# Rotary embedding in a transformer layer: the sine product and the value copy move from VectorE to GpSimd

## The reference

```
q = q * cos + rotate_half(q) * sin     # rotate_half: pairs (a, b) -> (-b, a)
k = k * cos + rotate_half(k) * sin
scores = q @ k.T / sqrt(8); softmax; @ v; then @ Wo + bo
```

## Time and profile before

| | |
|---|---|
| median of 3 runs | 843.28 us |
| lowest and highest | 841.11 and 844.68 us |
| span of the profiled execution | 841.5 us |
| TensorE busy | 740.7 us (88%) |
| VectorE busy | 460.5 us (55%) |
| ScalarE busy | 373.8 us (44%) |
| GpSimd busy | 188.6 us (22%) |

### The profile page before, as it was taken

How to read it: one execution, slowest core, us unless ns; L and a number is a source line. 1 busy time by engine, 2 the same in 40 slices (tenths; PEclk the granted TensorE clock), 3 DMA queues, 4 the chain that set the end, 5 groups by cost and what they waited for, 6 DMA issues and landing times.

```text
span 841.5 us, 13291 instructions
## 1 busy us (share of the span) xinstructions
PE 740.7 (88%) x4776; PEld 393.5 (47%) x4776; DVE 460.5 (55%) x942; ACT 373.8 (44%) x569; POOL 188.6 (22%) x158
## 2 busy tenths in 40 slices
PE   4547999999998588999999999996645999999998
PEld 2224656566565333333343444543323565665655
DVE  6314554555456987799978887645313333333334
ACT  6213334344343747646666676776202232222322
POOL 1017333433434513000000000001013333333332
PEclk9877999999998679999999999997967999999999
DMA  5794444434430000000000000000694222122122
GB/s 167 40 29 138 137 122 114 123 113 122 120 89 26 1 1 1 1 1 1 1 2 1 1 2 1 1 2 1 19 28 90 69 75 75 50 75 75 55 70 76
DMA packets 16169, 44.37 MB, mean 53 GB/s; under 512 B 2658, under 2 KB 5090, under 8 KB 16132
## 3 DMA queue, kind: packets, MB, share of 16 engines
q1 hardware_dynamic: 12388, 33.65, 21.2%
q10 hardware_dynamic: 3744, 10.23, 4.0%
HBM read 40.58 MB, written 1.19 MB: 50 GB/s over the span
## 4 chain that ended last, share of the span: by engine, by line
PE 78%; DMA 8%; DVE 6%; ACT 4%; SPq 2%; issue 1%; POOL 1%; DVEq 0%; ACTq 0%; POOLq 0%
PE psum L861 49%; PE psum L1025 8%; DMA R<-oT 8%; PE psum L1009 7%; PE psum L998 7%; PE psum L996 2%; SPq L361 2%; PE psum L1012 2%; DVE m_part L811 2%; PE psum L983 1%; ACT kT L567 1%; ACT xT L474 1%; PE psum L1032 1%; DMA x_res<-x_dram 1%; DVE kaug L801 0%
## 5 line engine op out<-in xcount | busy, mean ns | idle before, releaser
L861 PE MATMUL psum<-xT,W_hi 128*128 128x512 f16 x880 | 266.3, 385 | 0.0
L383 POOL TENSOR_TENSOR R<-R 128x512 f32<-128x512 f32 x112 | 151.4, 1354 | 346.2 <-DVE R L722 237.5
L861 PE MATMUL psum<-W_hi,R 128*128 (+1 forms) x896 | 168.9, 278 | 53.9 <-DVE R L722 53.9
L811 DVE TENSOR_REDUCE m_part<-psum 128x1 f32<-128x512 f32 (+3 forms) x384 | 188.2, 551 | 42.3 <-PE psum L998 40.0
L708 DVE SCALAR_TENSOR_TENSOR R<-psum,R 128x512 f32<-128x512 f32 x108 | 74.6, 691 | 209.5 <-ACT R L495 209.5
L495 ACT ACTIVATE R<-psum 128x512 f32<-128x512 f32 x108 | 64.3, 596 | 246.9 <-PE psum L861 246.9
L582 ACT ACTIVATE R<-psum 128x1024 f32<-128x1024 f32 x144 | 141.8, 1024 | 68.1 <-PE psum L1009 45.7
L861 PE MATMUL psum<-xT,W_lo 128*128 128x512 f16 x440 | 168.5, 383 | 0.0
L861 PEld LDWEIGHTS psum<-xT,W_hi 128*128 (+1 forms) x880 | 87.1, 99 | 83.9 <-issue 4.2
L861 PEld LDWEIGHTS psum<-W_hi,R 128*128 128x128 f16 x896 | 89.1, 99 | 78.6 <-issue 37.2
L861 PE MATMUL psum<-W_lo,R 128*128 (+1 forms) x448 | 124.5, 278 | 0.0
(11 more groups left out here) (101 smaller groups left out, 456.4 us busy)
## 6 DMA issues: line engine op xcount, KB each, us to landing
R<-coef_dram SPq DMA_DIRECT2D x60, 256.0 KB, 3.9
w_stage<-w_dram ACTq DMA_DIRECT2D x26, 384.0 KB, 3.0
R<-coef_dram SPq DMA_DIRECT2D x8, 448.0 KB, 3.5
R<-coef_dram SPq DMA_DIRECT2D x8, 384.0 KB, 3.4
R<-coef_dram SPq DMA_DIRECT2D x6, 320.0 KB, 3.5
R<-coef_dram SPq DMA_DIRECT2D x6, 192.0 KB, 3.8
x_res<-x_dram SPq DMA_DIRECT2D x8, 128.0 KB, 2.2
R<-oT SPq DMA_DIRECT2D x4, 256.0 KB, 16.7
```

The costliest lines, as they stand in the source:

```text
L383: nc.gpsimd.tensor_tensor(hc[:, c, :], v[:, j, c, :], C[:, j, c * CH:(c + 1) * CH], ALU.mult).then_inc(s_hc[c], 1)
L811: nc.vector.tensor_reduce(m_part[:, h, kc:kc + 1], ps[:, 0:n], axis=AX.X, op=ALU.max).then_inc(free_of(e), 1)
L861: ins = nc.tensor.matmul(o, stat(a, k), mov(b, k), start=first and n == 0, stop=last and n == 3 * k_parts - 1, **kw)
```

## The change

GpSimd makes the product with the sine (pairs exchanged) itself, in front of the one with the cosine, and copies the values behind its addition. VectorE keeps the eviction with the bias, and its eviction waits for the copy of the values two tiles earlier (`s_vals`), which comes behind the rotation, in place of `s_rot`. GpSimd waits for its own memset of `qaug` (`s_ready` at 2) ahead of the first tile; VectorE's wait for `s_ready` at 1 goes. The planner's costs of `pj` become 0.6 for VectorE and 3.6 for GpSimd, from 1.2 and 1.8. With these figures the planner's list differs in 22 of its 721 places, all between the 37th and the 61st.

```diff
--- before.py
+++ after.py
@@ -110,7 +110,7 @@
         if kind == "va":
             return [(DVE, 3.2)], []
         if kind == "pj":
-            return [(PE, 1.0), (DVE, 1.2), (POOL, 1.8)], [("sp", t - 2)]
+            return [(PE, 1.0), (DVE, 0.6), (POOL, 3.6)], [("sp", t - 2)]
         if kind == "sp":
             return [(ACTE, 0.9), (DVE, 0.7)], [("pj", t)]
         if kind == "kx":
@@ -424,11 +424,17 @@
             for c in range(NC):
                 pool.wait_ge(s_y[c], MT)
             nc.gpsimd.memset(qaug[:, :, :, 24:32], 0.0).then_inc(s_ready, 1)
+            pool.wait_ge(s_ready, 2)
             for t in range(TT):
 
                 taken(pool, ("pj", t))
                 if t >= 2:
                     pool.wait_ge(s_qklo, t - 1)
+                x = qkv[:, t % 2, 0:QW + KW].rearrange("p (h n e) -> p h n e", n=HD // 2, e=2)
+                sin = rope[:, 1, t, :].rearrange("p (n e) -> p n e", e=2).unsqueeze(1)\
+                    .to_broadcast([P, NH + NKV, HD // 2, 2])
+                nc.gpsimd.tensor_tensor(rot_b[:, t % 2].rearrange("p (h n e) -> p h n e", n=HD // 2, e=2),
+                                        x[:, :, :, ::-1], sin, ALU.mult).then_inc(s_swap, 1)
                 cos = rope[:, 0, t, :].unsqueeze(1).to_broadcast([P, NH + NKV, HD])
                 ra = rot_a[:, t % 2, :]
                 nc.gpsimd.tensor_tensor(ra.rearrange("p (h d) -> p h d", d=HD),
@@ -437,6 +443,9 @@
                 pool.wait_ge(s_pool, 2 + t)
                 pool.wait_ge(s_swap, t + 1)
                 nc.gpsimd.tensor_tensor(ra, ra, rot_b[:, t % 2], ALU.add).then_inc(s_rot, 1)
+                nc.gpsimd.tensor_copy(vals[:, t, :, 0:HD],
+                                      qkv[:, t % 2, QW + KW:QKV].rearrange("p (h d) -> p h d", d=HD)
+                                      ).then_inc(s_vals, 1)
 
             pool.wait_ge(s_xn, 2 * TT)
             for t in range(TT):
@@ -777,22 +786,10 @@
                 elif kind == "pj":
                     ps = filled(dve, e)
                     if t >= 2:
-                        dve.wait_ge(s_rot, t - 1)
+                        dve.wait_ge(s_vals, t - 1)
                     nc.vector.scalar_tensor_tensor(out=qkv[:, t % 2, :], in0=ps[:, 0:QKV], scalar=1.0 / WS,
                                                    in1=bias[:, 0:QKV], op0=ALU.mult,
                                                    op1=ALU.add).then_inc(free_of(e), 1)
-                    taken(dve, e)
-                    if t == 0:
-                        dve.wait_ge(s_ready, 1)
-                    nc.vector.tensor_copy(vals[:, t, :, 0:HD],
-                                          qkv[:, t % 2, QW + KW:QKV].rearrange("p (h d) -> p h d", d=HD)
-                                          ).then_inc(s_vals, 1)
-
-                    x = qkv[:, t % 2, 0:QW + KW].rearrange("p (h n e) -> p h n e", n=HD // 2, e=2)
-                    sin = rope[:, 1, t, :].rearrange("p (n e) -> p n e", e=2).unsqueeze(1)\
-                        .to_broadcast([P, NH + NKV, HD // 2, 2])
-                    nc.vector.tensor_tensor(rot_b[:, t % 2].rearrange("p (h n e) -> p h n e", n=HD // 2, e=2),
-                                            x[:, :, :, ::-1], sin, ALU.mult).then_inc(s_swap, 1)
                 elif kind == "sp":
                     dve.wait_ge(s_qkhi, t + 1)
                     q = rot_a[:, t % 2, 0:QW].rearrange("p (h d) -> p h d", d=HD)
```

## The result

The changed kernel takes 846.29 us in the median of 13 runs (845.07 to 848.5), the kernel before 842.69 us in 13 runs beside it. The ratio is **1.0042 (95% interval 1.0032 to 1.0053)**: slower by 3.6 us, where +2.5 was forecast. The profiled execution spans 845.3 us against 841.5. On TensorE L967 and L980 are the transposes of keys and queries, L995 and L1006 the products for the maxima and the scores, L1022 the value product. (An experiment's own kernel can have other numbers for the same lines; the rows name the tiles.)

What follows compares the result with a forecast made beforehand. TensorE carries 78% of the chain of waits, VectorE 6%; the changed stretch is four stages with different limits. Terms 1.4 - 0.3 + 0 + 1.0 + 0.4 = +2.5 us on the median 843.28 gave 845.8 us, range 841.2 to 850.6.

Steps and rivals of the forecast that it cites:

- The opening: First tiles, up to the first row maximum: GpSimd replaces VectorE as the limit, first maximum at 296.5 us, +1.4 us.
- The pitch of 3.0: Opening stage: time per tile becomes 3.0 us against 2.90, set by GpSimd's four instructions in line plus contention.
- contention 0.25: Opening stage: GpSimd loses 0.25 us per tile to VectorE's two subtractions slipping between, bounds 0 to 0.63.
- The two rivals on GpSimd's price: Opening: reversed read dear, 1.74 us, total 850.3, chance 0.15; full exclusion, 0.63 us lost per tile, total 847.4, chance 0.13.
- Tile 6: Around 303 us: VectorE saves some 1.2 us, but ScalarE's line lets only 0.3 through to the query evacuation, -0.3 us.
- Tile 7: Around 317 us: VectorE's saved 1.2 us ends inside ScalarE's unbroken line up to the query evacuation, 0 us.
- The rival that put the time on the other side: Tiles 6 and 7: VectorE's relief sets the time because ScalarE has room, -2.75 us, total 840.5, chance 0.15.
- The order: Planner's places 37 to 61: second value product in front delays kx 4, +1.0 us; ends -0.7 and +1.1.
- The lower clock level: TensorE: lower clock lasting elsewhere than 306 to 310 us would show the prediction wrong; no term given.
- The bias add: Behind tile 7: GpSimd's bias add ends as VectorE's two subtractions come, lengthening them, +0.4 us; 0 to 0.9.
- The sum: Whole kernel: 1.4 - 0.3 + 0 + 1.0 + 0.4 = +2.5 us, giving 845.8 us; chance of this forecast 0.45.
- Everything behind keeps its order and moves along: Rest of the kernel behind the changed stretch: no further cost, so the span of 841.5 becomes 844.0 us.

Runs made afterwards that it cites:

- e1: The changed kernel with the planner's old costs for `pj`, so the old order of events; 1.0014 against the kernel before.
- e3: The changed kernel with GpSimd's sine product made a second time, into an unread buffer, for tiles 0 to 5; 1.0076 against the kernel before.
- e4: The kernel before, old order, with only tiles 6 and 7 rotated and their values copied as in the change; ratio 0.9997.
- e12: The kernel before, old order, with tiles 0 to 5 rotated by VectorE alone and tiles 6 and 7 by GpSimd alone; ratio 0.9974.
- e6: The kernel before, old order, with tiles 0 to 5 rotated by VectorE alone, tiles 6 and 7 shared as before; ratio 0.9987.
- e7: The kernel before with one planner event moved: the second value product ahead of m 31, `pj` 7 and kx 4; ratio 1.0023.
- e2: The kernel before with only the planner's new costs for `pj`, so the new order, rotation and copy still on VectorE; ratio 1.0026.
- e5: The kernel before, old order, with all eight tiles rotated by VectorE alone; ratio 1.0020.
- e8: The kernel before with the planner's new costs, but the second value product put back behind kx 4; ratio 1.0008.

## Why the prediction came out right

- **The opening** was forecast at +1.4 us and is +1.28 (17.91 - 16.63). The pitch of 3.0 was 2.97. Its parts: the sine product 0.82 by the step, 0.82 by the starts (285.31 to 286.13); contention 0.25, measured 1.09 - 0.87 = 0.22, all of it from L797, none in the addition. The two rivals on GpSimd's price fall by the same rows: 0.863 us for the reversed read, and 0.22 instead of 0.63 us lost to the turns. The 0.05 us by which an instruction starts ahead of its predecessor's recorded end was assumed; the eight bias adds quoted for it give 0.02 (5.84 - 5.70 over seven steps), and the rows after give 0.04 (286.17 against 286.13).
- **Tile 6**, -0.3: measured -0.26, in the change, e1, e3, e4 and e12 alike. A part of the relief went before ScalarE could hide it: L821, with 16 elements, took 0.88 us instead of 0.23 beside GpSimd's products. Of the 1.2 us TensorE's transposes got 0.63 (9.57 us behind the first maximum instead of 10.20), and ScalarE's line let 0.26 through.
- **Tile 7**, 0: measured 0.00 (3.98 in both). The rival that put the time on the other side stands on this step and is refuted by e4.
- **The order**, +1.0 with ends at -0.7 and +1.1, was mis-sized. The two profiles show 12.20 - 11.69 = +0.51, but the 11.69 holds 3.4 us of the lower clock. The same old order at the full clock took 10.66 (e6), the new one 12.20 three times over: **+1.5 us at equal clock**. About 1.1 us of that is the value product (1.10 in e7). The rest comes from the early score products, behind which the maxima's products stand, a half that the sum had at nothing. (Alone and at the lower clock the halves add 1.10 and 0.64 us, 0.2 more than both together at the full clock.) The timed runs give the order +2.2 (e2).
- **The lower clock level** was named in the prediction as what could make it wrong, and had no term. In the change it falls in the two stages ahead of m 32: +0.39 and +1.60 us (four score products and a value product alone 1.86 + 1.94 - 1.02 - 1.07 = 1.71). In the kernel before it falls at 337 us, and by 345 us 0.84 us net is paid back: m 32 is 3.88 us later in the trace (328.48 - 324.60), the value product behind that place 3.04 (348.30 - 345.26). The 3.88 and the 3.04 both hold 0.36 us that was there at the first eviction (278.87 - 278.51). With the 1.03 us that the kernel before loses in the kx 4 stage (11.69 - 10.66) the clock's net by 345 us is 0.39 + 1.60 - 0.84 - 1.03 = 0.12 us: in this stretch both profiles have 6.8 us of the lower level, in other places.
- **The bias add**, +0.4: wrong, it is 0. L452 ends at 322.82 + 5.52 = 328.34, and L797 comes at 329.68 with 0.41 us, undisturbed, because the lateness of everything else had grown past the 2.1 us reckoned.
- **The sum.** Up to 345 us the change costs 1.28 - 0.26 + 0 + 0.51 + 0.39 + 1.60 - 0.84 = 2.68 us, where +2.5 was forecast. Split by cause it is opening 1.28, tile 6 -0.26, order 1.54 at equal clock, clock 0.12, bias add 0. So the order was half a microsecond dearer than its term and the bias add 0.4 cheaper, and these two errors cancel by luck; the clock, unpriced, happened to cost nearly nothing up to here. (The 1.54 and the 1.03 rest on e6's one profile at the full clock.) "Everything behind keeps its order and moves along" did not hold to the end: TensorE's products of equal number are 3.04 us apart at 345 us, 3.3 from 400 to 550, 3.5 at 590 and 3.8 at the end, so 0.8 us more comes behind the change's own stretch. e2 shows the same, +1.6 us at 345 and +2.2 at the end, both counted from the first eviction. Part of it comes in the feed-forward part, where the lower level falls otherwise in the two profiles (granted 0.66 instead of 0.75 from 580 to 600 us). What causes it isn't shown.

What precedes the clock's fall in the rows: in the change TensorE waits 1.54 us and then 2.27 (at 320.96 and 324.06); in the kernel before, 1.09 and 1.61. The wider gap does not explain the fall: e4 and e12 have the same two gaps (0.44 and 2.26, 0.44 and 2.27), and e12 has the lower level there and e4 has not. All four profiles with the value product in front have the lower level ahead of m 32 (the change, e2, e3, e7). Of the seven in the table with it behind, three have it too (e1, e6, e12) and four haven't (before, e4, e5, e8). What places it stays open.

## What to carry to other kernels

Where two engines take turns at SBUF, as here (2.90 us shared, 2.50 by VectorE alone), a stage's pitch holds the work of both, and handing work to the slower one can lengthen it though the faster looks full of it. Look for a form whose best time is far under its median. Giving whole tiles to one engine helped only with the faster one in the opening (e6, e12), and only while the engine that was freed did not start something that collides (e5). A planner's cost figure is part of the change: here its two numbers cost about twice what the moved instructions did (+2.2 and +1.2 us, each within about 1 us), and they should be tried apart.

## What the runs showed of the hardware

GpSimd's 128x320 product with exchanged pairs took 863 ns against 869 for the plain one, and 128x64 copies 239 ns. A VectorE instruction of 16 elements with two SBUF inputs, L821, took 882 ns beside GpSimd and 229 alone. TensorE's lower clock level (granted 0.50) fell at different places in kernels that differ by a microsecond or two ahead of it, and the amount of it differed between executions of the same program: in 13 runs of the changed kernel the mean granted clock lay between 0.941 and 0.945, and the span between 846.7 and 843.2 us. The same old order took 10.66 us in the kx 4 stage at the full clock (e6) and 11.69 with 3.4 us at the lower one (before).
